# Delta-rule recurrence: leaf terms of the outputs summed on GpSimd before the centering products

## What is computed

```python
def step(S, t):                       # S: state of each head, 128 x 128
    q_t, k_t, v_t, a_t, b_t = t
    y = jnp.einsum('bhvk,bhk->bhv', S, k_t)
    err = y - v_t
    S = a_t[..., None] * S - (b_t[..., None] * err)[..., None] * k_t[:, :, None, :]
    o = jnp.einsum('bhvk,bhk->bhv', S, q_t)
    return (S, o)
...
o = _delta_scan(q, k, v, a, beta)
mu = jnp.mean(o, axis=-1, keepdims=True)
var = jnp.mean(jnp.square(o - mu), axis=-1, keepdims=True)
o = (o - mu) * jax.lax.rsqrt(var + LN_EPS) * ln_g + ln_b
g = jax.nn.sigmoid(x @ Wg).reshape(b, t, H, D)
o = (o * g).reshape(b, t, H * D)
return o @ Wo
```

## Time and profile before

| | us |
|---|---|
| median of 3 runs | 3316.79 |
| lowest, highest | 3305.04, 3324.02 |
| the profiled execution | 3323.35 |
| its span, first to last instruction | 3321.6 |
| recurrence within it, about | 670 to 2925 |

### The profile page before, as it was taken

The page is one execution under the profiler, slowest core; times in us unless marked ns, Lnnn a source line. Parts: engine busy times, 40 slices in busy tenths (PEclk is TensorE's granted clock), DMA queues, the critical chain, the costliest instruction groups (busy, mean ns, idle before and its releaser), DMA issues. The chain is left out here.

```text
span 3321.6 us, 47953 instructions
## 1 busy us (share of the span) xinstructions
PE 2941.5 (89%) x14232; PEld 2047.0 (62%) x14232; DVE 2412.1 (73%) x4820; ACT 1604.8 (48%) x3480; POOL 1287.5 (39%) x1455
## 2 busy tenths in 40 slices
PE   5999999478898898988988889898898988869999
PEld 2555555256666676766766667666676666635555
DVE  5777777477888888888888888888878888632332
ACT  3666666245555555455555555555555555411110
POOL 1666766523433444334444344433344333400000
PEclk9999999789999999999999999999999999979999
DMA  2565564632222322212222122221232222030000
GB/s 69 225 250 200 235 247 193 218 77 51 52 40 39 59 48 52 40 39 56 51 52 40 39 58 48 52 40 39 45 61 52 41 39 40 15 105 19 7 7 7
DMA packets 429785, 253.02 MB, mean 76 GB/s; under 512 B 400016, under 2 KB 412016, under 8 KB 414832
## 3 DMA queue, kind: packets, MB, share of 16 engines
q1 hardware_dynamic: 429568, 250.32, 27.4%
HBM read 145.31 MB, written 104.99 MB: 75 GB/s over the span
## 5 line engine op out<-in xcount | busy, mean ns | idle before, releaser
L245 DVE SCALAR_TENSOR_TENSOR A_acc<-A_psY,A_w,A_acc 128x410 f32<-128x410 f32 (+1 forms) x720 | 419.3, 637 | 156.0 <-ACT A_acc L285 156.0
L771 POOL TENSOR_TENSOR B_WT<-B_WT,B_G 128x128 f32<-128x128 f32 (+2 forms) x224 | 191.4, 854 | 779.2 <-issue 448.8
L1072 ACT ACTIVATE B_WL<-B_psT 128x128 f32<-128x128 f32 (+2 forms) x480 | 150.0, 313 | 530.6 <-PE B_psT L1489 530.6
L345 PE MATMUL A_psY<-A_xT,A_w 128*128 128x413 f32 (+1 forms) x960 | 347.2, 510 | 9.0 <-PE A_psAG L351 7.7
L202 POOL TENSOR_TENSOR A_outs<-A_outs,A_acc 128x410 f32<-128x410 f32 (+1 forms) x240 | 229.2, 986 | 254.0 <-ACT A_outs L293 254.0
L345 PEld LDWEIGHTS A_psY<-A_xT,A_w 128*128 128x128 f32 x960 | 180.2, 189 | 165.5 <-issue 164.2
L986 DVE TENSOR_TENSOR B_NC<-B_NC,B_psM 128x256 f32<-128x256 f32 x480 | 198.8, 414 | 113.6 <-PE B_psM L1516 94.7
L989 DVE TENSOR_REDUCE B_W<-B_NC 128x64 f32<-128x320 f32 x512 | 248.8, 486 | 17.6
L1516 PE MATMUL B_psM<-B_BD,B_WL 128*128 128x128 f32 x1536 | 238.1, 297 | 9.1
L285 ACT ACTIVATE A_acc<-A_psY,A_w 128x410 f32<-128x410 f32 (+1 forms) x240 | 166.0, 692 | 163.1 <-PE A_psY L345 161.5
L1516 PEld LDWEIGHTS B_psM<-B_BD,B_WL 128*128 128x128 f32 x1536 | 196.7, 198 | 75.4 <-ACT B_WL L1072 74.7
(11 more groups left out here) (197 smaller groups left out, 6926.4 us busy)
## 6 DMA issues: line engine op xcount, KB each, us to landing
scr<-A_outs SPq DMA_DIRECT2D x48, 1024.0 KB, 5.5
B_KQ<-scr SPq DMA_DIRECT2D x96, 512.0 KB, 6.6
scr<-A_outag SPq DMA_DIRECT2D x32, 1024.0 KB, 8.0
A_xc<-nbeta SPq DMA_DIRECT2D x18, 1024.0 KB, 8.6
scr<-A_x SPq DMA_DIRECT2D x16, 1024.0 KB, 7.6
B_A<-scr SPq DMA_DIRECT2D x32, 512.0 KB, 5.3
B_C<-scr SPq DMA_DIRECT2D x32, 512.0 KB, 4.6
B_G<-scr SPq DMA_DIRECT2D x32, 512.0 KB, 4.6
```

The source lines that it names most:

```text
L245: nc.vector.scalar_tensor_tensor(a, y, w[:, s, col:col + 1], a, ALU.mult, ALU.add)\
L345: last = nc.tensor.matmul(psY[p][:, y0:y0 + HALO + t1 - t0], wp[:, p, kt, :], xT[:, kt, t0:t1 + HALO], start=kt == 0, stop=kt == KT - 1)
L771: tt(dst, dst, gr, ALU.mult).then_inc(wsc.sem, 1)
L1072: copy = lambda out, in_: nc.scalar.activation(out, in_, ACT.Copy)
```

## The change

The rows of WX that belong together are summed on GpSimd first, in a new function `sum_y` of four additions: row 1 onto row 2; rows 3 and 5 onto rows 4 and 6; rows 7 and 8 onto rows 4 and 6; row 9 onto row 6. They stand in GpSimd's queue between its scalings: the first behind the last `decayed_q`, the second between `scale_right(g, 5)` and `scale_left(g, 5)`, the third and fourth behind `scale_left(g, 5)`. Each centering half is then two products, FQ and rows 0 and 2, or FQ and rows 4 and 6. The second half stands wholly behind leaf 7, where only its rest stood. It waits for the fifth y term before its first product (before: the fourth) and for the fourth addition before its second.

```diff
-            6: out and [("oc", 1)],
-            7: out and [("oc_rest", 1)],
+            7: out and [("oc", 1)],
...
+            def sum_y(o, n):
+
+                to, by = ((WX[:, 2], WX[:, 1]), (WX[:, 4:7:2], WX[:, 3:6:2]), (WX[:, 4:7:2], WX[:, 7:9]), (WX[:, 6], WX[:, 9]))[n]
+                wait(pool, yv, o, (2, 4, 5, 5)[n])
+                if n >= 2:
+                    wait(pool, ysum, o, n)
+                tt(to, to, by, ALU.add).then_inc(ysum.sem, 1)
...
                 scale_left(g, 3)
                 queries(3)
+                sums(0)
                 gates(2, 3)
                 scale_right(g, 5)
+                sums(1)
                 scale_left(g, 5)
+                sums(2, 3)
                 scale_right(g, 7)
...
                     wait(pe, fq, g - 1, 2 * n + 2)
-                    wait(pe, yv, g - 1, 4 if n else 2)
+                    wait(pe, yv, g - 1, 5 if n else 2)
                     mm(ps[:], center[:], FQ[:, 512 * n:512 * (n + 1)], start=True, stop=False)
-                    mm(ps[:], center[:], WX[:, 4 * n:4 * n + 3:2], start=False, stop=False)
-                    if n:
-                        return
-                    last = mm(ps[:, HJ:2 * HJ], center[:], WX[:, 1], start=False, stop=True)
+                    wait(pe, ysum, g - 1, 4 if n else 1)
+                    last = mm(ps[:], center[:], WX[:, 4 * n:4 * n + 3:2], start=False, stop=True)
...
-            def centered_rest(g):
-                b, _ = place[g, "oc", 1]
-                ps = ring[b]
-                wait(pe, yv, g - 1, 5)
-                mm(ps[:], center[:], WX[:, 3:6:2], start=False, stop=False)
-                mm(ps[:], center[:], WX[:, 7:9], start=False, stop=False)
-                mm(ps[:, HJ:2 * HJ], center[:], WX[:, 9], start=False, stop=True).then_inc(full[b], 1)
```

More of the change, by code:

```diff
@@ L390, in chunk_jobs @@
     for j in range(J):
-        jobs += [job for job in leaf_jobs(g, j) if job[0] != "oc_rest"]
+        jobs += leaf_jobs(g, j)
     return jobs + [("update", i) for i in range(4)]
@@ L523, in recurrence @@
         awm, wxc = Count(sem("decayed_w"), 6), Count(sem("w_rows_copied"), 1)
+        ysum = Count(sem("y_terms_summed"), 4)
         yv, fq = Count(sem("y_terms"), 5), Count(sem("fq_made"), 4)
@@ L776, in _ @@
                 queries = lambda *parts: [decayed_q(g - 1, n) for n in parts if g]
+                sums = lambda *parts: [sum_y(g - 1, n) for n in parts if g]
                 wait(pool, psc0, g, 1)
@@ L804, in _ @@
                 decayed_q(NCH - 1, n)
+            for n in range(4):
+                sum_y(NCH - 1, n)
             for n in range(4):
@@ L1520, in chunk @@
                     for job in leaf_jobs(g, j):
-                        if job[0] == "oc_rest":
-                            centered_rest(g)
-                        elif j == 14 or job[0] != "ktok":
+                        if j == 14 or job[0] != "ktok":
                             shared_job(g, job)
@@ L1543, in _ @@
                     shared_job(g, job)
-                    if job == ("oc", 1):
-                        centered_rest(g)
 def feed_forward(nc, ident, x_d, att_d, gate_d, gbias_d, wg_d, wu_d, wd_d, out_d):
```

## The result

The changed kernel takes 3361.06 us (median of 4 runs, 3359.38 to 3366.42) against 3320.40 for the kernel before (4 runs, 3305.04 to 3331.77). The ratio is 1.0124, with a 95% interval from 1.0097 to 1.0151: **slower by 1.2%, about 41 us**. The profiled execution has a span of 3358.5 us.

A forecast was written before the change was run, and what follows sets the result against it. DVE was taken as the path from the end of leaf 5 to the start of leaf 8. 3316.8 + 40 (DVE and GpSimd taking turns) + 10 (clock) = 3367 us; range for 8 in 10: 3312 to 3400.

The forecast's parts named there:

- the turns: DVE and GpSimd alternate whole instructions on SBUF operands; leaf 7's L986 comes 1.3 us late per chunk, +40 us.
- the clock: TensorE's clock falls should not become rarer; taken as +10 us, +25 if all 14 full-clock chunks fell.
- What bounds it: From the end of leaf 5 to the start of leaf 8 the path runs over DVE; removed TensorE work worth 0.
- the one at L991: DVE's L991 at leaf 6 loses its 0.6 us as before, now to an addition, ending 1462.48 instead of 1462.60.
- three DVE rows: DVE rows in leaves 5 to 8 said to be too long for their size, held by GpSimd; L991 0.88, L870 1.42.
- What DVE's rows were to show: Leaf 6's L947 at 0.7 us instead of 0.29, the first L870 at 1.8 instead of 0.85.
- Full-clock chunks of 67.7 and 71.3 us: Lengths forecast for chunks at full clock in the profile after; before, 66.4 and 69.95 us.
- Behind the last chunk: Additions end at 2901.8, the second centering product can end at 2902.7 against 2902.55 before: 0.
- TensorE as the path: Rival: shorter TensorE queues behind leaves 5 and 7 pay 0.43 each, -27 us, or -80 if all counts; chance 0.15.
- The turns cost no more than now: Rival: DVE slips its instructions into GpSimd's gaps, 0 to 0.5 us per chunk, 3310 to 3332 us; chance 0.15.
- The clock in every chunk: Rival: the clock falls in every chunk, +25 us on top of DVE's waits for GpSimd, 3382 us; chance 0.12.
- The late sum: Rival: sums come late and the second centering product waits for addition 4 behind leaf 7, some 3370 us; chance 0.02.

The follow-up runs named there:

- experiment 1: Changed kernel without its four GpSimd additions, so only the short centering products: 3319.60 us, ratio 0.9989.
- experiment 10: Kernel before, scale_right of leaf 7 moved ahead of scale_left of leaf 5, scale_left of leaf 7 behind scale_right of leaf 9: 3316.96 us.
- experiment 8: Changed kernel with the second centering half, two products, behind leaf 6 instead of leaf 7: 3358.45 us, ratio 1.0147.
- experiment 5: Changed kernel with additions 2 to 4 and then scale_right of leaf 7 all ahead of scale_left of leaf 5: 3326.65 us, ratio 1.0030.
- experiment 6: Changed kernel with additions 3 and 4 made a second time behind themselves: 3392.83 us, ratio 1.0226.
- experiment 2: The four additions as in the changed kernel, with the old products of the kernel before at their old places: 3355.45 us, ratio 1.0102.
- experiment 4: Changed kernel with additions 2, 3 and 4 all ahead of scale_left of leaf 5: 3338.47 us, ratio 1.0044.
- experiment 7: Changed kernel with additions 3 and 4 as plain copies of the second operand: 3346.51 us, ratio 1.0077.
- experiment 3: Changed kernel with additions 3 and 4 behind scale_right of leaf 7 instead of ahead of it: 3363.11 us, ratio 1.0125.

## Why the prediction was right

The forecast was 3367 us with +50 over the runs before; measured were 3361 and +41. That the two times are only 6 us apart is in part luck: the kernel before came out at 3320.4 instead of 3316.8 with its fourth run. The +50 was 40 for the turns and 10 for the clock; the steps give 31 x 1.14 = 35 and 31 x 0.13 = 4.

- **What bounds it: right.** The removed products were worth 0 at leaves 5, 6 and 7 each, as forecast (experiment 1). The page's 89% for TensorE would have misled; what told was that DVE's rows from 1460.74 to 1470.40 have no idle time and that L986 starts a microsecond after its operand. **Wrong for the last stretch:** DVE was to stay the path up to leaf 8, but there it now waits 0.94 us for TensorE at the lower clock.
- **The turns: right in kind, 1.14 us instead of 1.3.** The step that erred is the one at L991: it was to lose its 0.6 us as before. The additions wait for each other's completion, that leaves a gap of 0.15 us, and L991 (L1005 in the changed kernel) falls into it. The two errors, this one and the next, went opposite ways. Against that, the additions were longer than taken: 1.28 for the large one and 0.74 for the small, not 1.15 and 0.73, so 4.0 us per chunk and 133 us in the profile instead of 117. The Trainium skill's page "GPSIMD Engine Reference", section "Performance versus the Vector engine", gives about 2.6 cycles per element, from which the estimate was 1.2; that was nearer to the 1.28 than the row L761 was (1.03); L761 reads a broadcast second operand, and whether that makes the difference no run shows. The same page, section "Key points", says that GpSimd shares its SBUF interfaces with DVE, with contention against DVE instructions that have two SBUF inputs. The trace agrees, and shows for how long: up to the end of the GpSimd instruction that is running. The long L870 was rightly read as such a hold, but measured on an unequal pair: that of 1.42 us was set against a row of 0.85 with other operands. Free of GpSimd it takes 0.62 (experiment 10), so the hold was 0.8 us and not 0.6. And of the "three DVE rows" that the prediction announces it names two.
- **What DVE's rows were to show: half right.** L947 of leaf 6 at 0.45, forecast 0.7; the first L870 at 1.62, forecast 1.8; that the second L870 would also wait (1.40) was not in the reckoning, nor that GpSimd's own second half would be held (1.53).
- **The clock: the sign right, the place and the price wrong.** Falls were to become no rarer; they come in every chunk now. They were priced at +10 us, or +25 if in all chunks. They cost 0.13 us per chunk, some 4 us: falls at leaf 7 (0.89 per chunk) take the place of those at leaves 10 to 12 (0.82). The term took the falls to stay where they were and only to become more; instead a chunk with the early fall mostly has no late one (30 of 31 here, all 23 in experiment 8, 20 of 29 in experiment 1). Full-clock chunks of 67.7 and 71.3 us, which were forecast, don't exist.
- **Behind the last chunk: 0 forecast, 0.9 measured.** From the first centering product to the end of the last it is 7.1 us in TensorE's timeline of the changed kernel below, before 6.2 (2896.31 to 2902.55). Each half waits for GpSimd there. The four additions and the gaps between them took 4.2 us (2934.66 to 2938.88), not the 3.8 of the forecast.

```profile
2932.96 1.10 PE L1437 MATMUL B_ring<-B_SQ,B_center 128*128 128x512 f32 x2 [0.93 <-DVE B_WX L921]
2935.43 1.12 PE L1439 MATMUL B_ring<-B_WX,B_center 128*128 128x512 f32 x2 [1.38 <-POOL B_WX L740]
...
2938.93 1.13 PE L1439 MATMUL B_ring<-B_WX,B_center 128*128 128x512 f32 x2 [1.52 <-POOL B_WX L740]
```

- **The rivals.** TensorE as the path: refuted by experiment 1. "The turns cost no more than now": refuted for this place, but it is what one gets at another (experiment 5). The clock in every chunk: it happened, at a sixth of its price (4 us for 25). The late sum: didn't happen.

## What to carry to other kernels

An idle GpSimd isn't free beside DVE. Before moving elementwise work there, lay its place over DVE's timeline. In this kernel each GpSimd instruction in flight cost up to what was left of it where DVE ran instructions with two SBUF operands on the path; beside PSUM operands, or where DVE waited anyway, it cost next to nothing (0.03 us on the step in experiment 5). An engine with 89% busy time may still be one whose work can be cut for nothing: look for the engine whose rows have no idle time ahead of the step that others wait for, and for durations that differ between equal instructions.

## What was not expected of the hardware

- The turns are alternate in both directions: a GpSimd instruction that comes while DVE's is running waits as well (1.85 us for an addition of 1.28, experiment 6). So doubling the additions cost 0.67 us on the step instead of about 2.
- A gap of 0.15 us between two dependent GpSimd instructions is enough for a short DVE instruction to pass (L1005, 0.27 instead of 0.88).
- TensorE's clock at leaf 7 goes with the idle time before it, but not by that alone. Over the 31 chunks behind the first, the 512-column product L1508 (L1506, L1512) took 1.02 to 1.04 us in all chunks where 0.20 or 0.69 us of idle time stood ahead of leaf 7, in 13 of 31 with 1.94 (experiment 2), in 11 with 2.28 (experiment 8), in at most 2 with 2.60 to 2.78 (experiments 1, 4, 5 and 7), and in none with 3.08 or more (experiments 3 and 6, and the changed kernel).
- What the lower clock costs there can be read within one kernel, at the same idle time. In experiment 8 the step from leaf 7 to 8 was 5.20 us on average in the 11 chunks at full speed and 5.76 in the 10 with a product of 1.9; in experiment 1 it was 5.22 in 2 chunks and 5.93 in 23. At full speed it is the 5.21 of the kernel before, so the longer step is the clock's. What tips a chunk one way or the other at equal idle time isn't shown.
